# Seams between attention layers: last and first batches in merged steps, context sums on VectorE, residual behind the token split

## What is computed

```python
x = x + _L0_xattn_ref(_layernorm(x), ctx_1024, ...)   # l0x: 8 heads of 64, keys and values from ctx
x = x + _L0_ffn_ref(_layernorm(x), ...)               # l0f: causal attention, 16 heads of 64, rotary; l0m: 31 + 1 experts, top 3
x = x + _L1_xattn_ref(_layernorm(x), ctx_1024, ...)   # l1x: 16 heads of 8, keys and values from ctx
x = x + _L1_ffn_ref(_layernorm(x), ...)               # l1f: causal attention, 16 heads of 8, rotary; l1m: 8 experts, top 2
x = x + _L2_xattn_ref(_layernorm(x), ctx_1024, ...)   # l2x: x1 @ W1.T + mean over tokens of (ctx @ W2.T) + b
x = x + _L2_ffn_ref(_layernorm(x), ...)               # l2m: 32 + 1 experts
x = x + _L3_xattn_ref(...) ; x = x + _L3_ffn_ref(...) # l3x, l3m
```

## Time and profile before

| | us |
|---|---|
| median of 3 runs | 1477.8 (1473.95 to 1485.4) |
| profiled execution, whole | 1479.8 |
| its span, first to last instruction | 1478.0 |
| PE busy | 1272.7 (86%) |
| DVE busy | 954.9 (65%) |
| ACT busy | 742.8 (50%) |
| POOL busy | 463.2 (31%) |

### The profile page before, as it was taken

How to read it: one execution, slowest core, us unless ns; L and a number is a source line. 1 busy time by engine, 2 the same in 40 slices (tenths; PEclk the granted TensorE clock), 3 DMA queues, 4 the chain that set the end, 5 groups by cost and what they waited for, 6 DMA issues and landing times.

```text
span 1478.0 us, 29706 instructions
## 1 busy us (share of the span) xinstructions
PE 1272.7 (86%) x9739; PEld 920.4 (62%) x9782; DVE 954.9 (65%) x2171; ACT 742.8 (50%) x2136; POOL 463.2 (31%) x519
## 2 busy tenths in 40 slices
PE   3888789999987999997989799987998799998834
PEld 2767667777764566655777677764665565666513
DVE  2766366676668555566667666658666787556687
ACT  3667245565562344445777577762222242334574
POOL 6600156666654100014221322222001324774100
PEclk9999699999998999999999999998999899999977
DMA  8000000000001555551000000001224016560000
GB/s 274 8 7 22 1 1 1 0 0 0 0 2 65 164 189 191 191 175 36 1 0 0 1 2 0 0 2 45 79 78 142 1 29 156 161 158 27 1 0 29
DMA packets 37431, 82.80 MB, mean 56 GB/s; under 512 B 5074, under 2 KB 18514, under 8 KB 37236
## 3 DMA queue, kind: packets, MB, share of 16 engines
q1 hardware_dynamic: 37364, 81.94, 18.0%
HBM read 80.27 MB, written 1.64 MB: 55 GB/s over the span
## 4 chain that ended last, share of the span: by engine, by line
PE 61%; ACT 15%; DVE 12%; issue 7%; SPq 2%; DMA 1%; POOL 1%; ACTq 0%; DVEq 0%; POOLq 0%
PE score_bank L1427 15%; ACT h_all L924 10%; PE f_bank L1460 7%; PE f_bank L1211 5%; PE score_bank L1289 5%; PE turn_bank L1305 4%; PE turn_bank L1460 4%; PE out_bank L1460 3%; PE out_bank L1345 3%; PE out_bank L1314 2%; SPq L528 2%; PE score_bank L1280 2%; PE out_bank L1354 1%; DVE work L1778 1%; PE f_bank L1239 1%
## 5 line engine op out<-in xcount | busy, mean ns | idle before, releaser
L1427 PE MATMUL score_bank<-parts 128*128 128x512 f32 x1040 | 390.0, 497 | 6.1 <-DVE parts L1869 5.4
L924 ACT ACTIVATE h_all<-score_bank,top_score 128x128 f32<-128x128 f32 x896 | 282.4, 402 | 115.1 <-DVE top_score L1766 115.1
L1427 PEld LDWEIGHTS score_bank<-parts 128*128 128x128 f32 x1040 | 198.6, 192 | 157.5 <-issue 117.6
L1766 DVE TENSOR_REDUCE top_score<-score_bank 128x4 f32<-128x512 f32 x224 | 143.0, 682 | 137.7 <-PE score_bank L1289 137.7
L1460 PE MATMUL f_bank<-h_all,wset 128*128 128x512 f32 x260 | 137.8, 612 | 24.6 <-DVE h_all L1966 14.8
L1013 ACT ACTIVATE h_all<-score_bank,wset 128x512 f32<-128x512 f32 x128 | 87.9, 687 | 124.0 <-PE score_bank L1427 123.8
L1954 DVE TENSOR_TENSOR h_all<-work,h_all 128x512 f32<-128x512 f32 x124 | 88.9, 718 | 87.2 <-ACT h_all L1013 87.0
L1305 PE MATMUL turn_bank<-CF,h_all 128*128 128x128 f32 x512 | 83.3, 286 | 42.7 <-DVE work L1778 23.0
L702 POOL TENSOR_TENSOR small<-small,half_neg 128x4 f32<-128x4 f32 (+4 forms) x25 | 37.7, 1509 | 257.3 <-DVE small L1739 129.3
L1305 PEld LDWEIGHTS turn_bank<-CF,h_all 128*128 128x128 f32 x512 | 56.0, 143 | 69.0 <-ACT h_all L924 23.0
L1009 ACT ACTIVATE rope_c<-score_bank 128x512 f32<-128x512 f32 x66 | 39.4, 598 | 115.5 <-PE score_bank L1427 102.4
(11 more groups left out here) (398 smaller groups left out, 2610.6 us busy)
## 6 DMA issues: line engine op xcount, KB each, us to landing
work<-gates_l0m SPq DMA_DIRECT2D x62, 512.0 KB, 3.7
W0X<-gates_l2m SPq DMA_DIRECT2D x32, 256.0 KB, 3.9
CTX<-gates_l2m SPq DMA_DIRECT2D x32, 256.0 KB, 3.9
wset<-in_l0m SPq DMA_DIRECT2D x32, 128.5 KB, 3.5
W0X<-gates_l1m SPq DMA_DIRECT2D x8, 512.0 KB, 3.7
wset<-in_l1m SPq DMA_DIRECT2D x8, 384.0 KB, 3.2
CTX<-gates_l1m SPq DMA_DIRECT2D x6, 512.0 KB, 3.7
big<-in_w0f SPq DMA_DIRECT2D x4, 512.0 KB, 8.0
```

The costliest lines, as they stand in the source:

```text
L924: last = act.activation(held[c][:, P * m:P * m + P], score_bank[c][:, P * m:P * m + P], ACT.Exp, bias=top_score[c][:, m:m + 1], **sums)
L1427: last = pe_.matmul(bk[:, :], wt[s % 2][:, col:col + P], y[:, x], start=(part == 0), stop=(part == len(parts_of) - 1))
L1766: dve.tensor_reduce(top_score[c][:, :], split(score_bank[c][:, :], HEADS), AX_X, ALU.max, negate=True)\
```

## The change

- `batches` becomes `two_layers`, which writes two following layers out together. Step s of the first and step s - `JOIN` of the second are issued as one for the last five steps (13 to 17) of the first, their work sorted by its place in each list as a fraction of the list's length. With 17 for l0x, l0f's steps -2, -1 and 0 fall on l0x's 15, 16 and 17. With 16 for l1x, l1f's -2 to 1 fall on 14 to 17. The loops over steps 3 to 12 stay.
- The first part of the second layer's variances is taken ahead of step 14 of the first, the second part behind step 17; POOL takes the second roots ahead of the second layer's step 2, where it also scales the context sums and fills `V8`.
- Waits of the first batches are set to the other layer's last ones (buffers of queries, keys and values).
- The context sums are made on DVE, one reduction of `cT` for each batch ("CS", right behind the maxima), and PE's F3 of l0x waits for that of its batch. The product with `WL2` moves behind l0m's router, the copy of its result on ACT behind l0m's exponentials.
- `residual` waits for the split of all four groups in place of the gates.

```diff
--- before.py
+++ after.py
@@ -39,6 +39,8 @@
...
+JOIN = {"l0x": 17, "l1x": 16}
...
@@ -50,7 +52,7 @@
...
-        DVE=[("M", 0, "own"), ("M", 1, "own"), ("OP", 0, "before"), ("N", 0, "own"), ("C", 0, "last"), ("C", 1, "last"),
+        DVE=[("M", 0, "own"), ("M", 1, "own"), ("CS", 0, "next"), ("OP", 0, "before"), ("N", 0, "own"), ("C", 0, "last"), ("C", 1, "last"),
...
@@ -86,7 +88,7 @@
...
-    dict(name="l0m", steps=32, group=4, halves=1, gated=False, up=P, wcols=2 * P + 1, gates=32, front=4),
+    dict(name="l0m", steps=32, group=4, halves=1, gated=False, up=P, wcols=2 * P + 1, gates=32, front=5),
...
@@ -364,7 +366,7 @@
...
-        for name, uses in [("l0x", 4 * B), ("csum", 2), ("l0f", 7 * B), ("l0m", 5), ("l1x", 4 * B), ("l1f", 4 * B),
+        for name, uses in [("l0x", 4 * B), ("l0f", 7 * B), ("l0m", 6), ("l1x", 4 * B), ("l1f", 4 * B),
...
@@ -424,38 +426,42 @@
...
-        def batches(eng, kind, n, do, after_first=None, after_second=None, before_last=None, ahead_of={}):
...
+        def two_layers(eng, kind, n1, do1, n2, do2, ahead={}, after={}):
...
+            def work_of(n, do, own):
+                order = ORDER[n][kind]
+                return [(j / len(order), do, what, u, own + AWAY[whose]) for j, (what, u, whose) in enumerate(order)
+                        if 0 <= own + AWAY[whose] < B]
+            def steps(*layers):
+                for n, _, own in layers:
+                    if (n, own) in ahead:
+                        ahead[n, own]()
+                for _, do, what, u, b in sorted((w for n, do, own in layers for w in work_of(n, do, own)), key=lambda w: w[0]):
+                    do(what, u, b // 2, b % 2)
+                for n, _, own in layers:
+                    if (n, own) in after:
+                        after[n, own]()
+            def middle(n, do):
+                with eng.Fori(1, (B - 3) // 2) as i:
+                    for own in (1, 2):
+                        for what, u, whose in ORDER[n][kind]:
+                            do(what, u, i, own + AWAY[whose])
+            for own in range(-2, 3):
+                steps((n1, do1, own))
+            middle(n1, do1)
+            for own in range(B - 3, B + 2):
+                steps((n1, do1, own), (n2, do2, own - JOIN[n1]))
+            for own in range(B + 2 - JOIN[n1], 3):
+                steps((n2, do2, own))
+            middle(n2, do2)
+            for own in range(B - 3, B + 2):
+                steps((n2, do2, own))
...
@@ -728,14 +734,18 @@
...
-                        pool.wait_ge(scored, unit_no(L, i, s, 0) - L["units"])
+                        if isinstance(i, int) and 2 * i + s < 2:
+                            pool.wait_ge(scored, unit_no(LAYERS[0], PAIRS - 1, s, 0) + LAYERS[0]["units"])
+                        else:
+                            pool.wait_ge(scored, unit_no(L, i, s, 0) - L["units"])
...
@@ -770,12 +780,13 @@
...
-                batches(pool, "POOL", n, do)
+                return do
...
-                pool.wait_ge(step(name + ".gates"), 1)
+                pool.wait_ge(y_split, CHUNKS * stage_no[name] + CHUNKS)
...
-            power("l0f")
-            for s in range(2):
-                pool.memset(V8[s][:, :, 8:9], 1.0)
-                pool.memset(V8[s][:, :, 9:32], 0.0)
-            attention(LAYERS[1])
+            power("l0f", 0)
+            def later_tokens(n):
+                power(n, 1)
+                pool.wait_ge(rooted, part_at[n] + 2)
+            def behind_first():
+                later_tokens("l0f")
+                pool.tensor_scalar(csum[:, :], csum[:, :], 1.0 / P, None, ALU.mult).then_inc(step("csum.scaled"), 1)
+                for s in range(2):
+                    pool.memset(V8[s][:, :, 8:9], 1.0)
+                    pool.memset(V8[s][:, :, 9:32], 0.0)
+            two_layers(pool, "POOL", "l0x", attention(LAYERS[0]), "l0f", attention(LAYERS[1]), ahead={("l0f", 2): behind_first})
...
-            attention(LAYERS[2])
-            attention(LAYERS[3])
+            two_layers(pool, "POOL", "l1x", attention(LAYERS[2]), "l1f", attention(LAYERS[3]),
+                       ahead={("l1f", 2): lambda: later_tokens("l1f")})
...
-            r, k = front_use("csum", 1)
+            r, k = front_use("l0m", 4)
...
@@ -1038,11 +1061,6 @@
...
-            def context_sums():
-                r, k = front_use("csum", 0)
-                act.wait_ge(f_full[r], k + 1)
-                act.activation(csum[:, :], f_bank[r][:, 0:B], ACT.Copy, scale=1.0 / P).then_inc(f_drained[r], 1)
...
@@ -1050,17 +1068,15 @@
...
-            attention(LAYERS[0], after_second=sines, ahead_of={B: context_sums})
-            r, k = front_use("csum", 1)
+            two_layers(act, "ACT", "l0x", attention(LAYERS[0]), "l0f", attention(LAYERS[1]), after={("l0x", 0): sines})
...
+            two_layers(act, "ACT", "l0x", attention(LAYERS[0]), "l0f", attention(LAYERS[1]), after={("l0x", 0): sines})
+            turned_stream("l0m", scale=vec["gamma2"])
+            exponentials("l0m", 31)
+            r, k = front_use("l0m", 4)
             act.wait_ge(f_full[r], k + 1)
...
@@ -1229,6 +1245,8 @@
...
+                            pe_.wait_ge(csum_made, 2 * i + s + 1)
...
@@ -1495,36 +1516,23 @@
...
-            def context_sums():
-                pe_.wait_ge(in_w1, 16 * 4)
-                bk, full = front_begin("csum", 0)
-                for b in range(B):
-                    last = pe_.matmul(bk[:, b:b + 1], CTX[:, b, :], part_one, start=True, stop=True)
-                last.then_inc(full, 1)
-            def context_rows_of():
-                r, k = front_use("csum", 0)
-                pe_.wait_ge(f_drained[r], k + 1)
-                bk, full = front_begin("csum", 1)
-                pe_.matmul(bk[0:B, 0:P], csum[:, 0:B], WL2[:, P:2 * P], start=True, stop=False)
-                pe_.matmul(bk[0:B, 0:P], ones_row[:, 0:B], bo["l2x"], start=False, stop=True).then_inc(full, 1)
...
+            two_layers(pe_, "PE", "l0x", attention(LAYERS[0]), "l0f", attention(LAYERS[1]))
...
+            pe_.wait_ge(in_w1, 16 * 4)
+            pe_.wait_ge(step("csum.scaled"), 1)
+            bk, full = front_begin("l0m", 4)
+            pe_.matmul(bk[0:B, 0:P], csum[:, 0:B], WL2[:, P:2 * P], start=True, stop=False)
+            pe_.matmul(bk[0:B, 0:P], ones_row[:, 0:B], bo["l2x"], start=False, stop=True).then_inc(full, 1)
...
@@ -1802,8 +1810,16 @@
...
+                    if what == "CS":
+                        dve.wait_ge(cT_ready[slot], 16 * (s // 2 + 1) + 16 * i)
+                        dve.tensor_reduce(col(csum, b), cT[slot][:, :], AX_X, ALU.add).then_inc(csum_made, 1)
                     if what == "Y":
+                        if n == "l0f" and isinstance(b, int) and b == 0:
...
@@ -2035,11 +2044,13 @@
...
+            powered("l0x", 0)
+            two_layers(dve, "DVE", "l0x", attention(LAYERS[0]), "l0f", attention(LAYERS[1]),
+                       ahead={("l0x", B - 2): lambda: variances("l0f", 0), ("l0f", B - 1): lambda: variances("l0m", 0),
+                              ("l0f", B): lambda: normalise("l0m", AO, False, range(3))},
+                       after={("l0x", 0): lambda: powered("l0x", 1), ("l0x", B + 1): lambda: variances("l0f", 1),
+                              ("l0f", 2): lambda: powered("l0f", 1)})
+            variances("l0m", 1)
...
+            two_layers(dve, "DVE", "l1x", attention(LAYERS[2]), "l1f", attention(LAYERS[3]),
+                       ahead={("l1x", B - 2): lambda: variances("l1f", 0), ("l1f", B - 1): lambda: variances("l1m", 0),
+                              ("l1f", B + 1): lambda: normalise("l1m", AO, False, range(3))},
+                       after={("l1x", B + 1): lambda: variances("l1f", 1)})
+            variances("l1m", 1)
...
```

## The result

The changed kernel takes 1434.2 us (median of 4 runs, 1431.2 to 1436.1) against 1478.8 us (4 runs, 1474.0 to 1485.4) for the kernel before, measured beside it: a ratio of 0.9694, 95% interval 0.9652 to 0.9736. The forecast was 1442.9 us in a range of 1429 to 1461. The time saved is 44.5 us where 34.9 were forecast. The profiled execution has a span of 1434.3 us (1436.1 with what lies around it).

The account below looks back on a forecast made before the run. TensorE was taken as the bound (61% of the chain), with time to win where it idles or runs slowly; 20.2 + 7.2 + 3.9 + 4.2 - 0.3 - 0.3 = 34.9 us off 1477.8 gave 1442.9 us, range 1429 to 1461.

Parts of the forecast that it names:

- S0 of l0f: Scores of batch 0 in l0f; forecast about 20 us after S15, the scores of batch 15, of l0x.
- First seam: Passage from l0x to l0f, 42.3 us between scores; overlapping the two layers was to save 20.2 us.
- The list walk: PE's instructions timed in order through merged steps 15 and 16 at full clock: 20.1 us, 22.2 saved.
- a short fall: Allowance in the first seam for PE's granted clock dropping again: 2 us off the 22.2 saved.
- the step after S0: Normal l0f step after the first seam, 16.3 us at clock 0.90; gets OP15 in addition, no change forecast.
- The rival that the clock stays low: First seam: step 16 runs at 1.2 GHz until S0; 8.2 us less saved, 1451 us, chance 0.13.
- Second seam: Passage from l1x to l1f: two merged steps take 18.5 us in place of 25.7, 7.2 saved.
- Context sums: Sixteen DVE reductions in l0x of 0.29 us each, mostly hidden in DVE's 0.39 us wait for ACT: 0.3 us lost.
- The slower rival: l0x: each sum at the head of DVE's queue waits for its transfer or POOL; 1496 us, chance 0.04.
- Residual: POOL's residual behind the token splitting after both routers: 3.9 us saved in l0m, 4.2 in l1m.
- the late preparation in l1m: DVE's next preparation in l1m falls under POOL's spreading of rows, under which a cast took 3.74 us.
- late roots: l0f: POOL's roots, scaling and fills, about 2.3 us, ahead of step 2: 0.3 us lost, bounds 0 and 2.3.

Follow-up runs that it names:

- e4_tables_out: Kernel before the change, with only ScalarE's steps 1 and 2 of l0x put ahead of its loop: 1470.9 us, ratio 0.9953.
- e8_residual_alone: Kernel before the change, with only the residual's wait moved behind the splitting: 1470.4 us, ratio 0.9935.

## Why the prediction was right, and where it missed

**The direction and the mechanisms.** Faster by over 1% had 0.93. Every part moved the way it was argued: S0 of l0f 19.7 us after S15 (20.1 forecast), S1 of l1f 18.1 after S15 of l1x (18.5), splitting at 1.4 us a group everywhere, gate products at 1.7 us under POOL in l0m.

**First seam, 20.2 forecast, 23.6 measured.** The list walk was right to 0.4 us (22.2 forecast at full clock, 22.6 measured). The term that was mis-sized is the allowance for the clock: "I take a short fall, 2 us". The stretch shows 1.00, no fall at all. This is in part luck of the profiled execution: with the same join, two later traces do show a short fall, of 1.5 us, and for them the allowance was nearly right. A second term, the step after S0, "nothing", gave 1.2 us: it had a clock of 0.90 before and 1.00 after. That too hangs on the one execution, as e4_tables_out and e8_residual_alone, with this seam as before, have 1.00 and 14.9 us there. Together these are most of the 3.4 us by which the whole seam was undersized, over a third of the miss of 8.8 us between the spans. The rival that the clock stays low is answered by the row above; the experiment with the layers apart shows that it is low (0.70 over the seam) where the overlap is taken away, products or not. Keeping it up was the larger half of what the overlap gave (8.4 of 14.9 us), and the prediction had it as a risk to be allowed for.

**Second seam, 7.2 forecast, 7.4 measured** (7.6 by the stretch that the prediction used, 25.7 to 18.1). Right, and shown by undoing it.

**Context sums, 0.3 forecast, 0.6 measured.** Steps of 8.04 us against 7.97 without the sums, but only nine of them in the changed kernel, as the two steps before S15 take 7.97 there too; the expectations had counted thirteen, 0.85. Over the whole of S2 to S15 the cost can't be read: eight traces with the sums took 104.3 to 106.6 us, three without 104.8 to 105.0. A sum takes 0.28 us, so three quarters of it lie in the wait that was named. The Trainium skill's statement that a reduction doesn't block against GpSimd (SBUF — State Buffer, Who interferes with whom) can now be held against rows of the changed kernel, DVE and POOL in order of time:

```profile
34.74 2.84 POOL L843 TENSOR_SCALAR Y<-Y,ROWS 128x1024 f32<-128x1024 f32 x1 [0.27 <-POOL TAB L834]
35.38 0.29 DVE L1816 TENSOR_REDUCE csum<-cT 128x1 f32<-128x128 f32 x1 [3.65 <-DMA cT<-in_ctxT]
```

All sixteen take 0.27 to 0.29 us, beside POOL or not: the trace agrees. The slower rival, a sum at the head of DVE's queue, needed 3.1 us a step; the one long wait for a transfer (3.65 us) lies at the start of the layer, and S2 is no later than it was.

**Residual, 3.9 and 4.2 forecast, 4.5 and 4.5 between the traces, 3.8 to 4.5 and 4.1 to 4.2 by experiment.** Right in both halves, the late preparation in l1m included (3.23 us where 3.74 was taken).

**What was not in the sum.** The table loads, 4.5 us on the path: the 3.9 us that l0x gained and the 0.6 that the sums took of it (six long steps of 8.83 us against 7.97 give 5.1; e4_tables_out gained 5.7; what l0x gained is 2.8 to 5.1 us over the eight traces, whose first steps differ). This was the largest miss, and both of its halves were readable: the alternation 8.8 and 8.0 in the trace, which I had seen and took for the loop's rhythm, and in the diff the bound of the loop. I had costed what was added to and removed from l0x, and not that its loop now begins elsewhere. On the other side l0f's tail lost 1.6 us and l1x won 1.0. The tail's loss is no effect of the change: it also stands in e4_tables_out and e8_residual_alone, which differ from the kernel before only elsewhere, with a clock of 0.95 over the tail each time, and nine traces of kernels made from the changed one have 33.6 us as before. The gain in l1x is one: 132.6 to 132.9 us in all eleven traces with the new driver, 133.5 to 133.7 in the three without. Its cause stays open. 34.9 + 3.4 for the first seam + 4.5 for the loads - 0.3 for the sums + 0.9 for the residual + 0.2 for the second seam - 0.6 for tail and l1x, and some tenths in the late roots and the rest, which came out better by 0.7 together, make the 43.7 us.

## What to carry to other kernels

When a driver of loops is rewritten, read what stands in front of each loop on each engine: here the function table that was in place on entry decided what every turn loaded again, and peeling one turn more paid by itself. An overlap of two stages can be worth more than the idle time it fills, where a drained PE is granted the lower clock as in this seam (0.70), so cost both ways from rows at either clock. Two streams that are merged by a key change their common order when either gets an entry more or less: take an entry's work out and leave the entry, if the work is what is to be measured.

## What the runs showed that I had not expected

- A table load of 1.28 us on ScalarE, hidden from the list of the costliest groups by its small total (7 in 1478 us), cost 0.86 us of the path each time it ran in the loop.
- The seam's granted clock goes with how much the two layers overlap: 0.67 to 0.70 apart, 0.87 at join 18, 0.92 to 1.00 at join 17 with the sums, with nearly the same instructions. Behind l1m's gates it is 0.58 to 0.60 in the three traces with the residual ahead and 0.79 to 0.94 in the nine with it behind; with the spreading moved as well it was 1.00 once and 0.79 once. PE's longest wait there fell from 8.1 to 2.65 us and then to 1.3.
- The same program had l0f's tail at 0.59 in one execution and at 1.00 in another. A difference of 7 us between two kernels of 1435 us can be no more than that, and one of the wrong turns above began there.
